# A MetaFormer block on one core: image loops written out, two biases folded into weights and outputs, the second norm derived from the first, and one probability product moved to GpSimd

## The chip, the core and the metric

The kernel runs on one core of a Trainium2 chip. A core has five engines that run side by side and meet at semaphores: TensorE (PE, its weight loads are PEld), VectorE (DVE), ScalarE (ACT), GpSimd (POOL) and SyncE (SP), which here issues transfers. The metric is the device time of one execution in microseconds (us). The time of the kernel before is the median of three runs.

## What is computed

Four images of 128 channels and 32 x 32 pixels pass through a token mixer with three attention branches and then through a mixture of eight experts, two for each token.

```python
# per image; xs is the layer-normed image as 1024 tokens x 128 channels, 4 heads
q_c, k_c, v_c = xs @ qkv_cmp_w + b                      # compressed branch
k_cmp = mlp(unfold(k_c, 4, stride 2) + pos_embed)       # 225 blocks of 16 pixels
v_cmp = mlp(unfold(v_c, 4, stride 2))
attn_cmp = softmax(q_c @ k_cmp.T * SCALE);  out_cmp = attn_cmp @ v_cmp @ proj + b
idx = top_k(attn_cmp.sum(heads).mean(queries), 16)      # selected branch: 16 of the blocks
attn_slc = softmax(q_s @ k_s[idx].T * SCALE); out_slc = attn_slc @ v_s[idx] @ proj + b
out_win = window_attention(x, 7 x 7 windows, bias table) # 25 windows of 49 pixels
out = g0 * out_cmp + g1 * out_slc + g2 * out_win         # g = sigmoid(mlp(xs))
# then, over all 4096 tokens: layer norm, router, layer norm of that again,
# the two best of 8 experts (128 -> 512 -> 128, gelu), weighted sum, residual
```

## The kernel before

**Structure.** Each engine has its own program. The mixer is worked off image by image. `attention` holds three stages: the compressed branch in 8 tiles of 128 queries against 225 keys (the `"c"` tiles), the windows together with the choice of the 16 blocks, and the selected branch in 8 tiles against 256 keys (the `"s"` tiles). `seam` joins two images: it finishes image b (outputs of the branches, their projection and gated sum, two norms, router, places of the tokens) and at the same time does the head of image b + 1 (norm, projections, the two block MLPs of keys and values, window values). The order is: the opening seam (head of image 0), then three times attention and seam, then attention and seam of the last image, then the experts, then the sum. In the kernel before, attention and seam of the images 0 to 2 are the body of a hardware loop (`Fori`) on each engine, and the last image is written out behind it. I count images from 0 here.

**A tile of attention.** TensorE makes the scores of tile t in two PSUM banks (L1354). VectorE takes the maximum (`maxima`, L887). ScalarE makes the exponentials with their sums (L668). VectorE takes the reciprocal (L894) and multiplies each head's 225 or 256 columns (`divide`, four instructions, L897). TensorE transposes the probabilities (L1272), VectorE and ScalarE each copy one half out (`first_chunk`, L912 in the selected branch, and L683), and two products a branch use the copies (L1297). The order on TensorE is scores(t), transposes(t - 2), and at t = 6 the first output product. The order on VectorE is `maxima(t)`, `divide(t - 1)`, `first_chunk(t - 2)`. The probabilities lie in a ring of three buffers.

**Banks.** A plan gives each PSUM result a bank and a turn. A wait on `bank_full` means that TensorE has filled it, a wait on `bank_read` that it has been copied.

**The seam.** The keys' MLP has 16 positions. VectorE adds the position's embedding to a strided view of the keys and writes it to `kp` (L1096, 16 instructions), and TensorE multiplies `kp` (L1481). The values' MLP reads the strided view of `vcT` directly (L1330). The window values get their bias on VectorE (L1059). `normalise` is statistics, their aggregate, a power on GpSimd (L552) and the scaling (L865). It runs three times in a middle seam: for the next image, for the tokens, and for the tokens once more. The last matrix step is the keys' second layer (L1514), which ScalarE copies to the block-diagonal `kbd` (L779). TensorE ends the seam with waits for all banks, and the first scores of the next image need `kbd`.

**GpSimd.** It does the window softmax's subtraction and product (L582, L589), part of the gather, the powers, and the 16 scatters of an image (L607), which stand at the end of its turn.

## Time and profile before

| | |
|---|---|
| median of three runs | 875.09 us (874.01 to 877.78) |
| the profiled execution, its own time | 872.5 us |
| span of its trace | 870.7 us |
| busy PE, DVE, ACT, POOL | 662.6, 594.7, 414.1, 240.5 us |
| images (from the opening to the last place of a token) | up to some 665 us |
| experts and sum | the rest |

The span is the trace from the first to the last instruction. The busy time of an engine is the sum over its instructions, and says nothing on whether the others wait for it. For that the trace lists, before each instruction, how long the engine was idle and who released it. "issue" stands for an idle time in which the profile shows nothing that the engine waited for.

### The profile page before, as it was taken

The page shows a single profiled execution, that of the slowest core. Times are in us where ns is not written, and L with a number is a line of the kernel's source. Part 1 is how long each engine was busy: PE and PEld are TensorE (multiplying, and loading weights), DVE is VectorE, ACT ScalarE, POOL GpSimd, SP SyncE. Part 2 cuts the span into 40 slices and gives each one's busy share as a digit, 9 for nine tenths or more (in the row PEclk, how much of TensorE's full clock was granted, in tenths as well). Part 3 has the DMA queues.
Part 4 walks back from the last instruction along what each step waited for, and adds up shares of the span by engine and source line. Part 5 has one row for each costly group of instructions (what it writes and reads, how often), then busy time and mean ns, then how long its engine had stood idle before and what let it go on. Part 6 is the DMA issues. An engine that isn't in the chain of part 4 may idle for free. (4 is left out here: it accounts for less than half of the span.)

```text
span 870.7 us, 18341 instructions
## 1 busy us (share of the span) xinstructions
PE 662.6 (76%) x4992; PEld 503.3 (58%) x4993; DVE 594.7 (68%) x1930; ACT 414.1 (48%) x1203; POOL 240.5 (28%) x399
## 2 busy tenths in 40 slices
PE   3997777799677769977767898776752299999953
PEld 2694353569434346954434597444342299999952
DVE  4647868788598879859787887886965044444424
ACT  1327437334463543427355423733701188887852
POOL 5000230200434001133400211531003455555540
PEclk9999969899899799989989999896975599999985
DMA  9700000000100000000000000100022122222236
GB/s 320 229 1 0 3 5 0 26 24 1 34 19 5 1 25 3 23 24 29 5 1 1 1 25 7 44 23 7 0 105 54 56 58 67 67 64 64 66 116 220
DMA packets 34225, 39.66 MB, mean 46 GB/s; under 512 B 11246, under 2 KB 26720, under 8 KB 33888
## 3 DMA queue, kind: packets, MB, share of 16 engines
q1 hardware_dynamic: 28592, 27.73, 10.4%
q0 software_dynamic: 4416, 9.00, 3.1%
q10 hardware_dynamic: 1152, 2.10, 0.7%
q8 instruction: 36, 0.59, 0.3%
q14 instruction: 29, 0.24, 0.1%
HBM read 25.38 MB, written 14.50 MB: 46 GB/s over the span
## 5 line engine op out<-in xcount | busy, mean ns | idle before, releaser
L668 ACT ACTIVATE r_P<-ps,nmx 128x225 f32<-128x225 f32 (+1 forms) x192 | 85.9, 465 | 56.7 <-DVE nmx L887 56.7
L804 ACT ACTIVATE R<-ps,R 128x128 f32<-128x128 f32 x292 | 83.5, 368 | 45.0 <-PE ps L1565 45.0
L887 DVE TENSOR_REDUCE nmx<-ps 128x4 f32<-128x900 f32 (+1 forms) x64 | 73.8, 1155 | 35.0 <-PE ps L1354 34.9
L1272 PE MATMUL ps<-ident,r_P 128*128 128x128 f32 (+1 forms) x384 | 58.0, 296 | 44.8 <-DVE r_P L897 36.5
L1354 PE MATMUL ps<-kbd,qT 64*128 64x450 f32 (+1 forms) x256 | 80.0, 729 | 16.0 <-issue 16.0
L607 POOL DMA_INDIRECT xs_d<-pay,pos x64 | 62.1, 970 | 103.0 <-DVE pos L1077 84.7
L1272 PEld LDWEIGHTS ps<-ident,r_P 128*128 128x128 f32 (+1 forms) x384 | 45.3, 155 | 75.9 <-DVE r_P L897 54.6
L643 POOL DMA_INDIRECT z_d<-R x72 | 69.4, 963 | 66.5 <-DVE R L1243 44.2
L552 POOL TENSOR_TENSOR rstd<-vpe,minus_half 128x8 f32<-128x8 f32 x12 | 19.8, 1650 | 238.8 <-DVE vpe L862 238.8
L1565 PE MATMUL ps<-R 128*128 128x128 f32 x584 | 79.2, 280 | 0.0
L1581 PE MATMUL ps<-fw_sb,R 128*128 x576 | 78.4, 279 | 0.0
L1565 PEld LDWEIGHTS ps<-R 128*128 128x128 f32 x584 | 72.7, 196 | 0.0
L1581 PEld LDWEIGHTS ps<-fw_sb,R 128*128 128x128 f32 x576 | 70.4, 193 | 2.3 <-issue 0.2
L1237 DVE TENSOR_TENSOR R<-ps,w1v_sb 128x128 f32<-128x128 f32 x72 | 21.0, 292 | 63.6 <-PE ps L1581 62.8
L897 DVE TENSOR_SCALAR r_P<-r_P,rZ 128x225 f32<-128x225 f32 (+1 forms) x192 | 54.6, 348 | 1.7
L796 ACT ACTIVATE R<-fw_sb 128x518 f32 x74 | 48.1, 650 | 12.7 <-DVE R L1219 12.6
L1330 PE MATMUL ps<-r_vc,w1v_sb 128*128 128x225 f32 x256 | 53.8, 367 | 0.0
L1403 PE MATMUL ps<-ident,r_P 113*49 113x113 f32 (+1 forms) x208 | 27.3, 279 | 32.3 <-POOL r_P L589 16.7
L1354 PEld LDWEIGHTS ps<-kbd,qT 64*128 64x128 f32 x256 | 27.5, 225 | 40.1 <-issue 37.3
L1481 PE MATMUL ps<-r_kp,w1k_sb 128*128 128x225 f32 x256 | 49.8, 354 | 1.1 <-DVE kbdw L412 1.1
L1330 PEld LDWEIGHTS ps<-r_vc,w1v_sb 128*128 128x128 f32 x256 | 47.6, 188 | 4.1
L1481 PEld LDWEIGHTS ps<-r_kp,w1k_sb 128*128 128x128 f32 x256 | 48.2, 190 | 1.6 <-issue 1.4
(208 smaller groups left out, 1348.4 us busy)
## 6 DMA issues: line engine op xcount, KB each, us to landing
R<-xs_d SPq DMA_DIRECT2D x76, 65.0 KB, 1.8
kbdw<-z_d SPq DMA_DIRECT2D x8, 512.0 KB, 5.7
x_sb<-x SPq DMA_DIRECT2D x4, 512.0 KB, 3.3
w1k_sb<-w1k SPq DMA_DIRECT2D x1, 2048.0 KB, 10.2
w1v_sb<-w1v SPq DMA_DIRECT2D x1, 2048.0 KB, 14.7
fw_sb<-fw SPq DMA_DIRECT2D x1, 2048.0 KB, 10.6
fw_sb<-fw SPq DMA_DIRECT2D x4, 512.0 KB, 11.3
t_d<-r_P SPq DMA_DIRECT2D x4, 512.0 KB, 2.6
```

What stands on the lines that cost most here:

```text
L607: gp.indirect_dma_start(xs_d, bass.IndirectOffsetOnAxis(pos[:, NT * k + t:NT * k + t + 1], 0), pay[:, k, t, :], None).then_inc(scattered, 16)
L643: gp.indirect_dma_start(z_d, bass.IndirectOffsetOnAxis(wd[:, r, 1:2].bitcast(U32), 0), yrow[:, r, :], None).then_inc(y_out[r], 16)
L668: last = sc.activation(Pb[t % NRING][:, h, 0:m], bank(ph, name)[:, (h % 2) * m:(h % 2) * m + m], ACT.Exp, bias=nmx[:, t % NRING, h:h + 1], ...
L804: last = sc.activation(hT[:, r % 2, c, :], hid(r)[:, C * c:C * c + C], ACT.Gelu, bias=wx[:, r, O_B1 + c:O_B1 + c + 1])
L887: ve.tensor_reduce(nmx[:, t % NRING, :].rearrange("p (a h) -> p a h", a=2), v.rearrange("p a (h m) -> p a h m", h=2), AX.X, ALU.max, negat ...
L897: last = ve.tensor_scalar(v, v, rZ[:, t % NRING, h:h + 1], None, ALU.mult)
L1272: last = tr(bank(ph, name)[0:m, k * j:k * j + k], src, ident[0:k, 0:k])
L1330: last = mm(bank(ph, f"mv{a}")[:, 0:NB], w1v_sb[:, s, C * a:C * a + C], vcT[:, r:r + 2 * NBH - 1:2, c:c + 2 * NBH - 1:2], start=(s == 0), ...
L1354: mm(bank(ph, name)[:, 0:2 * mk], qT[p0:p0 + 64, 128 * t:128 * t + 128], kbd[p0:p0 + 64, 2 * k:2 * k + 2, 0:mk], start=True, stop=True)\
L1481: last = mm(bank(ph, f"mk{a}")[:, 0:NB], w1k_sb[:, s, C * a:C * a + C], kp[:, s, :], start=(s == 0), stop=(s == NPOS - 1))
L1565: last = mm(hid(r)[:, C * c:C * c + C], wx[:, r, C * c:C * c + C], xe[:, r % 2, :], start=True, stop=True)
L1581: last = mm(outputs(r), hT[:, r % 2, c, :], fw_sb[:, bass.ds(e, 1), W1X + C * c:W1X + C * c + C].rearrange("p a n -> p (a n)"), start=(c = ...
```

## The change

- **Loops.** The loops over the images are written out on all five engines. The expert loop stays a loop.
- **Embedding.** The embedding's product with the keys' first layer is made once, in the opening seam (banks `pb` and `pc`), and added to the bias of that layer (`b1k`). `kp` goes, and the keys' MLP reads the strided keys.
- **Window values.** Their bias is added to the window outputs instead (each row of the probabilities sums to one), and ScalarE copies the values out.
- **Second norm.** The statistics of the second token norm are not taken. Its factor is worked out on GpSimd from the first (`second_inverse_root`), and VectorE multiplies by it.
- **Selected branch.** VectorE takes only the reciprocal, and GpSimd multiplies all four heads in one instruction (`scale_selected`).

```diff
+    fill("pb", when=head and not attention)
+    fill("mk0", "mk1", when=head)
+    fill("pc", when=head and not attention)
...
+            def second_inverse_root(k, b):
+                inverse_root(k)
+                pool.wait_ge(rstd_ready, k + 1)
+                gp.tensor_tensor(var2[:, 0, :], rstd[:, :], mv[:, :, 1], ALU.mult).then_inc(rstd2_step, 1)
+                pool.wait_ge(rstd2_step, 4 * b + 1)
+                gp.tensor_tensor(var2[:, 1, :], var2[:, 0, :], rstd[:, :], ALU.mult).then_inc(rstd2_step, 1)
+                pool.wait_ge(rstd2_step, 4 * b + 2)
+                gp.tensor_scalar(var2[:, 0, :], var2[:, 1, :], EPS_T, None, ALU.add).then_inc(rstd2_step, 1)
+                pool.wait_ge(rstd2_step, 4 * b + 3)
+                gp.tensor_tensor(rstd2[:, :], var2[:, 0, :], minus_half[:, :], ALU.pow).then_inc(rstd2_step, 1)
...
+            def scale_selected(b):
+                for t in range(NT):
+                    pool.wait_ge(rz_ready, b * NT + t + 1)
+                    v = Pb[t % NRING][:, :, 0:256]
+                    gp.tensor_tensor(v, v, rZ[:, t % NRING, :].unsqueeze(2).to_broadcast([128, HEADS, 256]),
+                                     ALU.mult).then_inc(prob_ready, 1)
...
-            with pool.Fori(0, B - 1) as b:
+            for b in range(B - 1):
                 windows(b)
-                head(middle_one(b), b + 1, 3 * b + 1)
-                inverse_root(3 * b + 2)
-                inverse_root(3 * b + 3)
+                scale_selected(b)
+                head(middle_one(b), b + 1, 2 * b + 1)
+                second_inverse_root(2 * b + 2, b)
                 scatter_rows(b)
...
+                    for g in range(NGRP):
+                        n = min(4, NWIN - 4 * g)
+                        act.wait_ge(*filled(ph, f"vw{g}"))
+                        sc.activation(vw[:, 4 * g:4 * g + n, :].rearrange("p w c -> p (w c)"),
+                                      bank(ph, f"vw{g}")[0:WTOK, 0:n * C], ACT.Copy).then_inc(read_sem(ph, f"vw{g}"), 1)
...
                     dve.wait_ge(*copied(ph, f"S{s}{t}b"))
+                    if s == "s":
+                        ve.reciprocal(rZ[:, t % NRING, :], Z[:, t % NRING, :]).then_inc(rz_ready, 1)
+                        return
...
-                            last = ve.tensor_copy(
+                            last = ve.tensor_scalar(
                                 owT[:, :].rearrange("p (r c) -> p r c", c=W)[:, r0:r0 + nr, c0:c0 + ncol],
...
-                                .rearrange("p (r c) -> p r c", r=WS)[:, 0:nr, 0:ncol])
+                                .rearrange("p (r c) -> p r c", r=WS)[:, 0:nr, 0:ncol], col("bv_w"), None, ALU.add)
...
-                    for s in range(NPOS):
-                        r, c = divmod(s, KS)
-                        ve.tensor_scalar(kp[:, s, :].rearrange("p (r c) -> p r c", r=NBH),
-                                         kcT[:, r:r + 2 * NBH - 1:2, c:c + 2 * NBH - 1:2],
-                                         cols[:, COL_POS + s:COL_POS + s + 1], None, ALU.add).then_inc(kp_ready, 1)
...
-                    normalise(norm + 1, xt_tok, pay[:, 0, :, 0:C], EPS_T, xn_ready)
+                    dve.wait_ge(rstd2_step, 4 * t_ + 4)
+                    for t in range(NT):
+                        last = ve.tensor_scalar(pay[:, 0, t, 0:C], xt_tok[:, t, :], rstd2[:, t:t + 1], None, ALU.mult)
+                    last.then_inc(xn_ready, 1)
...
+                    if t_ is None:
+                        pe.wait_ge(*free_for(ph, "pb"))
+                        for i in range(NPOS // 4):
+                            for j in range(4):
+                                s = 4 * i + j
+                                last = mm(bank(ph, "pb")[32 * j:32 * j + 32, 0:2 * C], cols[:, COL_POS + s:COL_POS + s + 32],
+                                          w1k_sb[:, s, :], start=(i == 0), stop=(i == NPOS // 4 - 1))
+                        last.then_inc(full_sem(ph, "pb"), 1)
...
                     for s in range(NPOS):
-                        pe.wait_ge(kp_ready, h * NPOS + s + 1)
+                        r, c = divmod(s, KS)
                         for a in range(2):
-                            last = mm(bank(ph, f"mk{a}")[:, 0:NB], w1k_sb[:, s, C * a:C * a + C], kp[:, s, :],
+                            last = mm(bank(ph, f"mk{a}")[:, 0:NB], w1k_sb[:, s, C * a:C * a + C],
+                                      kcT[:, r:r + 2 * NBH - 1:2, c:c + 2 * NBH - 1:2],
                                       start=(s == 0), stop=(s == NPOS - 1))
```

Three places show how the order of the instructions moves. The first is ScalarE where the loop over the images begins, between the copy to `kbd` and the first exponentials of an image. Before:

```order
L779 ACTIVATE kbd<-ps,cols 32x225 x3
L786 UNCONDITIONAL_BRANCH
L786 ISA
L665 ISA [waits t_stored]
L668 ACT_TABLE_LOAD
L668 ACTIVATE r_P,Z<-ps,nmx 128x225 [waits max_ready]
L668 ACTIVATE r_P,Z<-ps,nmx 128x225 x3
```

After, at the same place of the image (L813 is the copy to `kbd`, L696 the exponential, L807 the window values):

```order
L807 ACTIVATE r_vw<-ps 49x128 [waits bank_full1]
L813 ACTIVATE kbd<-ps,cols 32x225 [waits bank_full2]
L813 ACTIVATE kbd<-ps,cols 32x225 x3
L696 ACT_TABLE_LOAD [waits max_ready]
L696 ACTIVATE r_P,Z<-ps,nmx 128x225 [waits t_stored]
L696 ACTIVATE r_P,Z<-ps,nmx 128x225 x3
```

The branch is gone, and the load of the activation table now stands behind the wait for the first maximum, in all four images. In the kernel before it stands there in the last image only.

The second place is VectorE in the middle of the selected branch: two tiles before (L887 maximum, L894 reciprocal, L897 product, L912 copy of the transposed half).

```order
L887 TENSOR_REDUCE nmx<-ps 128x4 [waits bank_full1,bank_full0]
L894 RECIPROCAL rZ<-Z 128x4 [waits bank_read7]
L849 REGISTER_ALU
L897 TENSOR_SCALAR r_P<-r_P,rZ 128x256 [waits dve_done]
L897 TENSOR_SCALAR r_P<-r_P,rZ 128x256 x3
L912 COPY R<-ps 128x4x128 [waits bank_full3]
L883 REGISTER_ALU
L887 TENSOR_REDUCE nmx<-ps 128x4 [waits bank_full7,bank_full6]
L894 RECIPROCAL rZ<-Z 128x4 [waits bank_read1]
```

After, with L921 for the maximum, L929 for the reciprocal and L949 for the copy:

```order
L921 TENSOR_REDUCE nmx<-ps 128x4 [waits bank_full1,bank_full0]
L929 RECIPROCAL rZ<-Z 128x4 [waits bank_read7]
L949 COPY R<-ps 128x4x128 [waits bank_full3]
L921 TENSOR_REDUCE nmx<-ps 128x4 [waits bank_full7,bank_full6]
L929 RECIPROCAL rZ<-Z 128x4 [waits bank_read1]
```

The products are gone from VectorE, and the reciprocal of tile t - 1 still stands behind the maximum of tile t.

The third place is TensorE in the opening seam after the change, from the gate (L1500) over the new products (L1511, L1530) and the keys' MLP (L1520) to the values' MLP (L1359).

```order
L1500 MATMUL ps<-gw_sb,r_gh 128x3 x7
L1511 MATMUL ps<-w1k_sb,cols 32x256 [waits bank_read3,wk_in]
L1511 MATMUL ps<-w1k_sb,cols 32x256 x15
L1520 MATMUL ps<-r_kc,w1k_sb 128x225 [waits bank_read5,bank_read4]
L1520 MATMUL ps<-r_kc,w1k_sb 128x225 x31
L1530 MATMUL ps<-cols,pos_rows 128x1 [waits bank_read6,bank_read3]
L1530 MATMUL ps<-cols,pos_rows 128x1
L1359 MATMUL ps<-r_vc,w1v_sb 128x225 [waits bank_read7,bank_read6,wv_in]
```

Before, the keys' MLP stood directly behind the gate there, with a wait for `kp_ready` at each position.

## Rows read from the trace of the kernel before

**Rows 1.** The page: busy time, share of the span and count.

```profile
PE 662.6 (76%) x4992; PEld 503.3 (58%) x4993; DVE 594.7 (68%) x1930; ACT 414.1 (48%) x1203; POOL 240.5 (28%) x399
```

**Rows 2.** Waits of TensorE: who for whom, us in total, times, longest.

```profile
PE ps L1272 <- DVE r_P L897: 36.5, 37, 4.5
```

**Rows 3.** Timeline, image 0, entry of the loop: start, us, engine, line; idle before.

```profile
66.85 1.81 ACT L779 ACTIVATE kbd<-ps,cols 32x225 f32<-32x225 f32 x4 [6.10 <-PE ps L1514]
...
69.94 4.25 PE L1354 MATMUL ps<-kbd,qT 64*128 64x450 f32 x12 [2.25 <-issue]
...
98.49 0.15 DVE L964 TENSOR_REDUCE impcol<-impacc 97x1 f32<-97x8 f32 x1
```

**Rows 4.** Timeline, image 1, behind the first back edge.

```profile
222.47 1.80 ACT L779 ACTIVATE kbd<-ps,cols 32x225 f32<-32x225 f32 x4 [6.10 <-PE ps L1514]
...
229.63 2.73 PE L1354 MATMUL ps<-kbd,qT 64*128 64x450 f32 x6 [5.92 <-issue]
...
259.49 0.15 DVE L964 TENSOR_REDUCE impcol<-impacc 97x1 f32<-97x8 f32 x1
```

**Rows 5.** Timeline, image 3, written out behind the loop.

```profile
536.96 1.81 ACT L779 ACTIVATE kbd<-ps,cols 32x225 f32<-32x225 f32 x4 [6.10 <-PE ps L1514]
...
540.17 2.54 PE L1354 MATMUL ps<-kbd,qT 64*128 64x450 f32 x12 [1.98 <-issue]
...
542.53 1.28 ACT L668 ACT_TABLE_LOAD   x1 [3.77 <-DVE nmx L887]
...
571.70 0.15 DVE L964 TENSOR_REDUCE impcol<-impacc 97x1 f32<-97x8 f32 x1
```

**Rows 6.** Timeline of VectorE, image 1, selected branch, tiles 5 to 7.

```profile
302.96 1.22 DVE L887 TENSOR_REDUCE nmx<-ps 128x4 f32<-128x1024 f32 x1
304.09 0.17 DVE L894 RECIPROCAL rZ<-Z 128x4 f32<-128x4 f32 x1
304.29 1.14 DVE L897 TENSOR_SCALAR r_P<-r_P,rZ 128x256 f32<-128x256 f32 x4
305.35 0.68 DVE L912 COPY R<-ps 128x512 f32<-128x512 f32 x1
305.95 1.22 DVE L887 TENSOR_REDUCE nmx<-ps 128x4 f32<-128x1024 f32 x1
...
309.78 1.23 DVE L887 TENSOR_REDUCE nmx<-ps 128x4 f32<-128x1024 f32 x1 [0.76 <-PE ps L1354]
```

**Rows 7.** Timeline of TensorE in the same stretch.

```profile
299.51 1.09 PE L1272 MATMUL ps<-ident,r_gh 128*128 128x128 f32 x8 [0.57 <-DVE r_gh L897]
300.53 1.13 PE L1354 MATMUL ps<-kbd,qT 64*128 64x512 f32 x4
...
306.68 1.92 PE L1297 MATMUL ps<-R,v_sb 128*32 128x512 f32 x16
308.54 1.13 PE L1354 MATMUL ps<-kbd,qT 64*128 64x512 f32 x4
```

**Rows 8.** Timeline, image 1, windows: products of GpSimd, and TensorE behind one.

```profile
265.42 0.84 POOL L589 TENSOR_TENSOR r_P<-r_P,rZw 113x392 f32<-113x392 f32 x1 [5.00 <-DVE rZw L943]
...
284.75 0.51 POOL L589 TENSOR_TENSOR r_P<-r_P,rZw 49x196 f32<-49x196 f32 x1 [4.21 <-DVE rZw L943]
...
266.41 0.75 PE L1403 MATMUL ps<-ident,r_P 113*49 113x113 f32 x6 [1.58 <-POOL r_P L589]
```

**Rows 9.** Timeline of TensorE, second middle seam.

```profile
339.37 2.98 PE L1278 MATMUL ps<-xwin,qkvw_sb 128*128 128x245 f32 x8 [1.36 <-DVE r_vc L1101]
...
344.27 12.45 PE L1481 MATMUL ps<-r_kp,w1k_sb 128*128 128x225 f32 x64 [0.23 <-DVE kbdw L412]
```

**Rows 10.** Groups by line and shape: busy us, mean ns; idle before.

```profile
L1330 PE MATMUL ps<-r_vc,w1v_sb 128*128 128x225 f32 x256 | 53.8, 367 | 0.0
L1481 PE MATMUL ps<-r_kp,w1k_sb 128*128 128x225 f32 x256 | 49.8, 354 | 1.1 <-DVE kbdw L412 1.1
L1101 DVE TENSOR_SCALAR r_vc<-ps,cols 128x512 f32<-128x512 f32 x8 | 5.6, 740 | 0.0
```

**Rows 11.** Timeline, last seam: the router on TensorE, its reader on VectorE.

```profile
652.41 3.55 PE L1502 MATMUL ps<-wr_sb,R 128*128 128x8 f32 x16 [0.73 <-ACT R L763]
...
656.95 0.22 DVE L1140 TENSOR_TENSOR lg<-ps,rows 128x64 f32<-128x64 f32 x1
```

More of the change, by code:

```diff
@@ L300, in build @@
         vpe = sb("vpe", [128, NT])
+        var2 = sb("var2", [128, 2, NT])
+        rstd2 = sb("rstd2", [128, NT])
         gtok = sb("gtok", [128, NT, 3])
@@ L468, in store_t @@
                 sp.wait_ge(t_ready, b + 1)
-                sp.dma_start(t_d[bass.ds(b, 1), :, :].rearrange("a p n -> (a p) n") if not isinstance(b, int) else t_d[b, :, :],
-                             r_P[:, 0:N]).then_inc(t_stored, 16)
+                sp.dma_start(t_d[b, :, :], r_P[:, 0:N]).then_inc(t_stored, 16)
             sp.wait_ge(*filled(opening(), "xt1"))
             sp.dma_start(x_sb[:, :], x[1, :, :]).then_inc(x_in, 16)
-            with sp.Fori(0, B - 2) as b:
+            for b in range(B - 2):
                 select_tokens(b)
                 sp.wait_ge(*filled(middle_one(b), "xt1"))
-                sp.dma_start(x_sb[:, :], x[bass.ds(b + 2, 1), :, :].rearrange("a p n -> (a p) n")).then_inc(x_in, 16)
+                sp.dma_start(x_sb[:, :], x[b + 2, :, :]).then_inc(x_in, 16)
                 store_t(b)
@@ L621, in _ @@
             windows(B - 1)
[L622 to L623 removed]
+            scale_selected(B - 1)
+            second_inverse_root(2 * B - 1, B - 1)
             scatter_rows(B - 1)
@@ L655, in hidden_units @@
             def hidden_units(ph, name, a):
-                h, bias = {"mk": (hk, "b1k"), "mv": (hv, "b1v")}[name]
+                h, bias = {"mk": (hk, b1k[:, a:a + 1]), "mv": (hv, col(f"b1v{a}"))}[name]
+                act.wait_ge(*copied(opening(), "pc"))
                 act.wait_ge(*filled(ph, f"{name}{a}"))
                 sc.activation(h[:, a, :], bank(ph, f"{name}{a}")[:, 0:NB], ACT.Gelu,
-                              bias=col(f"{bias}{a}")).then_inc(read_sem(ph, f"{name}{a}"), 1)
+                              bias=bias).then_inc(read_sem(ph, f"{name}{a}"), 1)
             def attention(ph, b):
@@ L785, in _ @@
             seam(opening(), None, 0)
-            with act.Fori(0, B - 1) as b:
+            for b in range(B - 1):
                 attention(middle_one(b), b)
@@ L1052, in combine @@
                             link(last)
-            def values(ph):
-                for g in range(NGRP):
-                    n = min(4, NWIN - 4 * g)
-                    dve.wait_ge(*filled(ph, f"vw{g}"))
-                    ve.tensor_tensor(vw[:, 4 * g:4 * g + n, :],
-                                     bank(ph, f"vw{g}")[0:WTOK, 0:n * C].rearrange("p (w c) -> p w c", c=C),
-                                     rows[0:WTOK, ROW_BVW:ROW_BVW + C].unsqueeze(1).to_broadcast([WTOK, n, C]),
-                                     ALU.add).then_inc(read_sem(ph, f"vw{g}"), 1)
             def rows_of_picks(ph):
@@ L1170, in seam @@
                 if h is not None:
-                    values(ph)
                     dve.wait_ge(*filled(ph, "v2"))
@@ L1181, in _ @@
             assert links[1] == LINKS_FIRST, links
-            with dve.Fori(0, B - 1) as b:
+            for b in range(B - 1):
                 links[0], links[1] = LINKS_FIRST + b * LINKS_MIDDLE, 0
                 attention(middle_one(b), b)
-                seam(middle_one(b), b, b + 1, 3 * b + 1)
+                seam(middle_one(b), b, b + 1, 2 * b + 1)
                 assert links[1] == LINKS_MIDDLE, links
@@ L1188, in _ @@
             attention(closing(), B - 1)
-            seam(closing(), B - 1, None, 3 * B - 2)
+            seam(closing(), B - 1, None, 2 * B - 1)
             done = [0]
@@ L1484, in seam @@
                                 last.then_inc(full_sem(ph, f"mk{a}"), 1)
+                    if t_ is None:
+                        pe.wait_ge(*copied(ph, "pb"))
+                        pe.wait_ge(*free_for(ph, "pc"))
+                        for a in range(2):
+                            last = mm(bank(ph, "pc")[:, a:a + 1], pos_rows[:, C * a:C * a + C], col("quads"),
+                                      start=True, stop=True)
+                        last.then_inc(full_sem(ph, "pc"), 1)
                 if t_ is not None:
@@ L1541, in _ @@
             seam(opening(), None, 0)
-            with pe.Fori(0, B - 1) as b:
+            for b in range(B - 1):
                 attention(middle_one(b), b, b + 1)
```

36 lines of the change are left out of this document (22 added, 14 removed).

## The prediction

> **What bounds the kernel now.** I read the page first: TensorE is busy for 76% of the span and VectorE for 68% [rows 1], so no engine alone is the bound, and each stage has to be read from its own waits. The waits of TensorE come next: its largest single one, 36.5 us, is for the probability product of VectorE [rows 2]. Then I read the timelines at the joints between images. In image 1 the copy to `kbd` ends at 224.27 and TensorE issues the next scores at 229.63, 5.4 us later, with no releaser [rows 4]. In images 0 and 3, which do not stand behind a back edge, the same gap is 1.3 and 1.4 us [rows 3, 5]. In the selected branch a tile takes 2.99 us (from the maximum at 302.96 to the next at 305.95), and VectorE has no gap in it: maximum, reciprocal, four products, copy [rows 6]. In the seam TensorE runs the two block MLPs with almost no idle time [rows 9]. So there are three regimes: VectorE in the tiles, TensorE in the seams, a stall at the joints.
>
> **The joints.** I compare one stretch in the images: from the end of the `kbd` copy to the last instruction of the compressed branch (L964). It is 98.49 - 68.66 = 29.8 us in image 0 [rows 3], 35.2 in image 1 [rows 4] and 571.70 - 538.77 = 32.9 in image 3 [rows 5]. Image 3 is already straight-line code, so it is the pattern for all four after the change. It is slower than image 0 for a reason that the order of instructions shows: the table load of 1.28 us stands behind the first maximum, at 542.53 [rows 5]. Beside it TensorE idles longer in the fill, and the scatters of the image before run beside its tiles. After the change all four images have the load there. The gap of 1.4 us contains a branch in image 3 that will be gone. The waits for the banks stay, so I take 0.5 us, between 0.1 (a plain semaphore) and 1.4. That gives 32.0 us for images 1 to 3, and 31.3 for image 0, which has no scatters beside it: 29.8 and the load of 1.3, some 1.0 for the longer idle time, less 0.8 of gap. Images 1 and 2 save 3.2 each (I take image 2 like image 1), image 3 saves 0.9, and image 0 loses 1.5. Sum: **-5.8 us**, bounds -2.2 (gap as now) to -8.5.
>
> The Trainium skill (Runtime: NRT & Kernel Launch, Instruction fetch mechanics) says that a taken branch out of the loaded pages has to fetch its target before it can go on. By it the two gaps would fall wholly, some 10 us; it does not count the table load.
>
> **The selected branch.** Off VectorE: four products, 1.05 us of pitch a tile [rows 6]. Onto GpSimd: one product of 1024 columns. The trace has 392 columns in 0.84 and 196 in 0.51 us [rows 8], hence 1.7 ns a column, and 0.51 + 828 x 0.0017 = 1.9 us. Bounds: 1.5 (if long rows run some 25% faster than these short ones of 49) to 2.4.
>
> Does the tile get shorter? The orders decide. TensorE issues scores(t) only behind transposes(t - 3), and VectorE the reciprocal(t - 1) only behind maximum(t). So there is a ring of two tiles: transposes to scores 1.02 (299.51 to 300.53), scores to maximum 1.24 (308.54 to 309.78), maximum to reciprocal 1.13 [rows 6, 7], reciprocal and hop 0.25, product 1.9, hop to TensorE 0.15 (266.26 to 266.41 [rows 8]). The sum is 5.7, or 2.86 a tile. With the product on VectorE the same ring has 1.4 behind the start of the reciprocal instead of 2.3, that is 2.4 a tile, and VectorE's own work (2.99) decides. The tile thus gets only 0.1 us shorter, while the product's latency shows at both ends: the first transposes come 0.9 later, and so do the last. The output product at t = 6 (1.86 us, 306.68 to 308.54 [rows 7]) falls between transposes(4) and scores(7). Before, slack took up most of it: the last maximum comes 3.83 instead of 2.99 behind the one before (305.95 to 309.78 [rows 6]). Now it falls into the ring whole. I went through the eight tiles with these steps, each instruction at the later of its input and its engine. With the product on VectorE this gives 6.83 us from maximum(5) to maximum(7); the rows say 6.82. With the product on GpSimd the transposes of tiles 0, 5 and 7 come 0.9, 0.9 and 1.45 later than before. So the stage is 1.45 us longer, **+5.8 us** for four images. At a product of 1.5 us it is 0.3 shorter an image (-1), at 2.4 it is 3.5 longer (+14).
>
> The Trainium skill (GPSIMD Engine Reference, 3.1 Elementwise) speaks against this edit: it has 4497 ns for 2048 columns with two inputs. As an estimate from that page the product would take 2.3 us and the sum would be 7 us higher. This trace is below the page's pace (0.84 us for 392 columns), so I stay with the rows.
>
> **The seams.** In a middle seam `kp` (16 instructions of VectorE) goes, and with it TensorE's waits of 1.36 and 0.23 [rows 9]. The MLP now streams strided keys. The values' MLP does that already, at 367 against 354 ns [rows 10], so 64 instructions cost 0.8 more. Net -0.7, x3: **-2.1**. What else leaves VectorE here (statistics, a wait for GpSimd, window values) stood beside TensorE's back-to-back work and is worth nothing. The window values on ScalarE fill an idle time of 6.10 us ahead of `kbd` [rows 3 to 5]; without that cover they would cost seven copies of 512 columns, some 4 us at the 0.68 of VectorE's [rows 6]. In the opening seam the path is TensorE, and it gains the embedding products: 32 instructions of 256 columns into 32 rows each, like the 16 of 512 that take 1.92 [rows 7], so 1.9; 0.8 for the stride; 0.3 for the small products. Sum **+3.0**, bounds 1 and 9 (the upper one if the four strips don't overlap).
>
> **The last seam.** VectorE's second norm ends some 4 us earlier. But the next thing that it needs is the router's product, which ends at 655.96, and its reader starts at 656.95 now [rows 11]. So only 0.9 is left: **-0.9**, bounds 0 and -2.7 (if the router runs at the full TensorE clock). The places, scatters and experts behind it are unchanged.
>
> **Window outputs.** 25 copies an image get a column operand. From 512 columns the two forms cost 0.74 and 0.68 [rows 6, 10], so up to 0.06 each, 1.4 of VectorE. The stage is a relay between four engines; I take a third to be on the path, 0.45 an image, **+1.8**, bounds 0 and 5.6.
>
> **Sum:** -5.8 + 5.8 - 2.1 + 3.0 - 0.9 + 1.8 = +1.8, against the profiled execution's own 872.5, that is 874.3. The median of the runs shown lies 2.6 above it, so I predict **877 us**. About 0.5% (4.4 us) is what a measurement of this kernel can tell from no change.
>
> **Rivals.**
> - *GpSimd's product is quick (faster).* At 1.5 us the ring has slack, the branch gives -1 instead of +5.8, and with the gap at 0.1 us the joints give 1.6 more: 877 - 8.4, about 868. For it: the rows only show short rows of 49 columns. Against: the slope from two points. It decides below some 1.6 us.
> - *GpSimd's product is slow (slower).* At 2.4 us the branch costs +14 and the kernel takes about 885. For it: two inputs from SBUF over 1024 columns. Against: VectorE here reads PSUM, and nothing beside GpSimd stretched its 0.84 us.
> - *The joint isn't the branch.* If the 5.4 us stay in straight code, because loading the code itself is late, the joints only lose: 877 + 6 to 8, about 884. Against: image 3 shows 1.4 us.
> - Not in the cases: the half-clock spells of TensorE fall elsewhere. They may move the time by 3 us either way and are in the range.
>
> **Chances.** Forecast 0.44, quick product 0.25, slow product 0.23, stall that stays 0.08. The forecast's own range is 872 to 881; the range that holds 8 in 10 goes to the two products, 867 to 886. The quick product counts as faster, the slow one and the staying stall as slower, and the forecast as the same.
>
> **What would show it.** The new product on GpSimd at 1.9 us with a tile of 2.9 us in the selected branch, and VectorE waiting in it for scores; the first scores of an image within 0.5 us of `kbd`, with the table load behind the first maximum; no wait before L1520, whose mean is some 367 ns; a router reader that waits for TensorE. The forecast is wrong if a tile of the selected branch falls below 2.6 us or rises above 3.1.

## The result and the profile after

| | before | after |
|---|---|---|
| median, us (5 runs each, one chip) | 875.37 | 879.07 |
| lowest to highest, us | 874.01 to 877.78 | 878.43 to 881.55 |
| ratio (95% interval) | 1 | 1.0049 (1.0027 to 1.0071) |
| profiled execution: time, span, us | 872.5, 870.7 | 878.4, 876.4 |

The change costs some 0.5%, at the edge of what a measurement of this kernel tells from nothing; in a second group of runs (the control below) the ratio was 1.0069 (1.0042 to 1.0096). The page's line of busy time, beside [rows 1], has VectorE 77 us lower and GpSimd 64 higher:

```profile
PE 672.8 (77%) x5028; PEld 506.9 (58%) x5029; DVE 517.7 (59%) x1644; ACT 427.3 (49%) x1231; POOL 304.0 (35%) x443
```

**The joint** of image 0 after, on the timeline (start, us, engine, line; idle before in brackets), beside [rows 3]:

```profile
68.41 1.81 ACT L813 ACTIVATE kbd<-ps,cols 32x225 f32<-32x225 f32 x4 [0.43 <-PE ps L1562]
...
71.23 1.03 PE L1383 MATMUL ps<-kbd,qT 64*128 64x450 f32 x4 [1.98 <-issue]
...
73.58 1.28 ACT L696 ACT_TABLE_LOAD   x1 [3.37 <-DVE nmx L921]
...
102.31 0.15 DVE L1001 TENSOR_REDUCE impcol<-impacc 97x1 f32<-97x8 f32 x1
```

The gap behind `kbd` is 71.23 - 70.22 = 1.0 us (1.1 in image 1, 1.0 in the others), not 5.4, and not the 0.5 that I took. The table load is where it was expected. From here on I take the stretch from the end of `kbd` to the end of the importance column just before L1001, which is 0.1 behind the start of L1001 that the prediction took. It takes 32.2, 32.8, 32.7 and 32.7 us, against 29.9, 35.3, 35.2 and 33.0 before [rows 3 to 5]. TensorE's queue has the gap in it. One line's instructions, after, in the window 69 to 72 us:

```profile
L1586 PEldq EVENT_SEMAPHORE  x9: 51/51/51, 70.3 to 71.1; - x9
```

and the line of the back edge in the kernel before, with its durations in ns (least, median, most):

```profile
L1542 PEldq COMPARE_BRANCH  x3: 83/3802/3916, 225.6 to 540.0; - x3
L1182 DVEq COMPARE_BRANCH  x3: 59/63/72, 224.8 to 539.3; - x3
```

The first of the nine records is the wait for `kbd` itself, and eight more stand behind it in the seam's list of banks. All banks but that one have been free before, but each wait takes 0.11 us of the queue ((71.13 - 70.25) / 8). So of the 5.4 us before, 1.2 were waits and some 3.9 the taken branch of TensorE; the same branch cost VectorE 0.06. The branch that was not taken, behind the third image of the loop, took 0.08. A taken branch is not dear in itself: the back edge of the experts' loop, whose body has some 180 records of TensorE where the images' has some 2000, takes TensorE 0.21 to 0.25 us (the least, 0.083, is the one that was not taken):

```profile
L1571 PEldq COMPARE_BRANCH  x18: 83/215/248, 701.2 to 838.8; - x18
```

**The ring** of the selected branch, image 1 after, beside [rows 6, 7]. VectorE, then GpSimd, then TensorE:

```profile
303.49 1.23 DVE L921 TENSOR_REDUCE nmx<-ps 128x4 f32<-128x1024 f32 x1 [0.20 <-PE ps L1383]
304.63 0.18 DVE L929 RECIPROCAL rZ<-Z 128x4 f32<-128x4 f32 x1
305.44 0.69 DVE L949 COPY R<-ps 128x512 f32<-128x512 f32 x1 [0.62 <-PE ps L1301]
307.04 1.22 DVE L921 TENSOR_REDUCE nmx<-ps 128x4 f32<-128x1024 f32 x1 [0.91 <-PE ps L1383]
...
309.13 1.22 DVE L921 TENSOR_REDUCE nmx<-ps 128x4 f32<-128x1024 f32 x1 [0.21 <-PE ps L1383]
...
314.52 1.23 DVE L921 TENSOR_REDUCE nmx<-ps 128x4 f32<-128x1024 f32 x1 [2.76 <-PE ps L1383]
```

```profile
304.89 1.89 POOL L625 TENSOR_TENSOR r_P<-r_P,rZ 128x1024 f32<-128x1024 f32 x1 [0.20 <-DVE rZ L929]
308.42 1.89 POOL L625 TENSOR_TENSOR r_P<-r_P,rZ 128x1024 f32<-128x1024 f32 x1 [1.64 <-DVE rZ L929]
```

```profile
297.48 1.85 PE L1301 MATMUL ps<-ident,r_P 128*128 128x128 f32 x8 [2.27 <-POOL r_P L625]
299.26 2.00 PE L1383 MATMUL ps<-kbd,qT 64*128 64x512 f32 x4
301.19 1.10 PE L1301 MATMUL ps<-ident,r_P 128*128 128x128 f32 x8
302.22 1.13 PE L1383 MATMUL ps<-kbd,qT 64*128 64x512 f32 x4
```

The product takes 1.89 us, two tiles take 309.13 - 303.49 = 5.64, and VectorE waits for scores in the ring. What the rows also show is a cost that the prediction left out: the scores of 299.26 take 2.00 us where others take 1.13, because TensorE's clock was granted at half there (1.2 instead of 2.4 GHz, behind an idle time of 2.27 for GpSimd). From the first maximum of the branch to the last it takes 22.1 to 22.5 us in the four images, against 20.3 to 20.4 before.

The four stretches from the first selected scores to the first norm of the result, image by image, before and then after (us; busy us and count of each engine; PEclk, the granted share of TensorE's clock; DMA share, GB/s):

```profile
129.40:164.70 35.30, 26.88 (x182) 15.65 (x175) 28.23 (x80) 21.80 (x76) 0.00 (x0) 0.91 0.05 16
287.30:321.70 34.40, 27.00 (x178) 14.92 (x175) 28.21 (x81) 21.80 (x76) 0.00 (x0) 0.92 0.05 16
443.70:479.20 35.50, 26.96 (x179) 16.01 (x175) 28.21 (x81) 21.80 (x76) 0.00 (x0) 0.92 0.00 1
601.40:646.40 45.00, 31.03 (x199) 17.94 (x194) 35.43 (x104) 20.71 (x74) 0.00 (x0) 0.88 0.03 13
```

```profile
132.40:169.00 36.60, 27.96 (x178) 15.75 (x175) 20.19 (x49) 21.61 (x76) 15.10 (x8) 0.89 0.05 15
289.80:326.80 37.00, 27.80 (x180) 15.92 (x175) 20.25 (x49) 21.58 (x76) 15.10 (x8) 0.89 0.04 15
446.30:482.90 36.60, 28.04 (x182) 15.76 (x175) 20.24 (x48) 21.69 (x76) 15.10 (x8) 0.89 0.00 0
603.40:651.40 48.00, 32.86 (x198) 19.21 (x194) 27.41 (x73) 20.57 (x74) 15.10 (x8) 0.82 0.03 12
```

VectorE does 8 us less in each, and each is longer: by 1.3, 2.6, 1.1 and 3.0, 8.0 in all. The granted clock is lower in all four.

**The seams.** TensorE in the first middle seam and in the opening (then the keys' first product in the opening before), and the two forms of the block MLP:

```profile
189.33 13.41 PE L1520 MATMUL ps<-r_kc,w1k_sb 128*128 128x225 f32 x64
```

```profile
32.94 1.93 PE L1511 MATMUL ps<-w1k_sb,cols 128*32 128x256 f32 x32
...
34.81 0.47 PE L1520 MATMUL ps<-r_kc,w1k_sb 128*128 128x225 f32 x1
```

```profile
34.72 12.42 PE L1481 MATMUL ps<-r_kp,w1k_sb 128*128 128x225 f32 x64 [0.36 <-DVE kbdw L412]
```

```profile
L1359 PE MATMUL ps<-r_vc,w1v_sb 128*128 128x225 f32 x256 | 54.0, 367 | 0.0
L1520 PE MATMUL ps<-r_kc,w1k_sb 128*128 128x225 f32 x256 | 53.7, 368 | 0.0
```

No wait stands ahead of L1520, and its mean is 368 ns. In the last seam the router's reader waits for TensorE:

```profile
657.38 3.55 PE L1550 MATMUL ps<-wr_sb,R 128*128 128x8 f32 x16 [0.73 <-ACT R L791]
...
660.97 0.22 DVE L1170 TENSOR_TENSOR lg<-ps,rows 128x64 f32<-128x64 f32 x1 [3.15 <-PE ps L1550]
```

### The profile page after: what moved, and what is told of

Its sections match the earlier page's. It is cut to its first block, busy times and chain, and to the rows that moved or that the text cites. A ratio compares the mean times of both kernels' runs of the same rounds, so it can differ in the third digit from the quotient of the medians.

```text
span 876.4 us, 17293 instructions
## 1 busy us (share of the span) xinstructions
PE 672.8 (77%) x5028; PEld 506.9 (58%) x5029; DVE 517.7 (59%) x1644; ACT 427.3 (49%) x1231; POOL 304.0 (35%) x443
## 4 chain that ended last, share of the span: by engine, by line
PE 51%; DVE 21%; POOL 9%; issue 7%; DMA 5%; ACT 4%; POOLq 1%; SPq 1%; DVEq 0%; ACTq 0%
PE ps L1307 7%; PE ps L1520 6%; PE ps L1359 6%; PE ps L1301 5%; DVE nmx L921 5%; PE ps L1383 5%; PE ps L1629 4%; PE ps L1613 4%; PE ps L1326 3%; ACT r_P L696 3%; POOL r_P L625 3%; PE ps L1350 3%; DVE r_P L934 3%; DMA R<-xs_d 2%; POOL xs_d L634 2%
## 5 line engine op out<-in xcount | busy, mean ns | idle before, releaser
L696 ACT ACTIVATE r_P<-ps,nmx 128x225 f32<-128x225 f32 (+1 forms) x192 | 86.0, 466 | 53.5 <-DVE nmx L921 53.5
L1301 PE MATMUL ps<-ident,r_P 128*128 128x128 f32 (+1 forms) x384 | 62.6, 312 | 53.3 <-DVE r_P L934 26.1
L921 DVE TENSOR_REDUCE nmx<-ps 128x4 f32<-128x900 f32 (+1 forms) x64 | 73.7, 1156 | 49.1 <-PE ps L1383 49.0
L1301 PEld LDWEIGHTS ps<-ident,r_P 128*128 128x128 f32 (+1 forms) x384 | 49.4, 167 | 86.8 <-DVE r_P L934 38.1
L1383 PE MATMUL ps<-kbd,qT 64*128 64x450 f32 (+1 forms) x256 | 82.6, 752 | 6.8 <-issue 3.6
L625 POOL TENSOR_TENSOR r_P<-r_P,rZ 128x1024 f32<-128x1024 f32 x24 | 45.3, 1893 | 53.2 <-DVE rZ L929 53.2
L601 POOL TENSOR_TENSOR r_gh<-r_gh,nmw 113x392 f32<-113x392 f32 (+1 forms) x20 | 15.5, 773 | 111.5 <-DVE nmw L969 111.3
L1359 PE MATMUL ps<-r_vc,w1v_sb 128*128 128x225 f32 x256 | 54.0, 367 | 0.0
L1520 PE MATMUL ps<-r_kc,w1k_sb 128*128 128x225 f32 x256 | 53.7, 368 | 0.0
L1432 PE MATMUL ps<-ident,r_P 113*49 113x113 f32 (+1 forms) x208 | 26.7, 275 | 31.4 <-DVE R L1028 17.2
L1520 PEld LDWEIGHTS ps<-r_kc,w1k_sb 128*128 128x128 f32 x256 | 47.8, 188 | 4.9 <-issue 0.4
L1359 PEld LDWEIGHTS ps<-r_vc,w1v_sb 128*128 128x128 f32 x256 | 47.6, 188 | 4.2
L1257 DVE TENSOR_SCALAR R<-ps,R 128x128 f32<-128x128 f32 x74 | 30.2, 408 | 28.4 <-PE ps L1608 21.1
```

What stands on the lines that cost most here:

```text
L625: gp.tensor_tensor(v, v, rZ[:, t % NRING, :].unsqueeze(2).to_broadcast([128, HEADS, 256]), ALU.mult).then_inc(prob_ready, 1)
L696: last = sc.activation(Pb[t % NRING][:, h, 0:m], bank(ph, name)[:, (h % 2) * m:(h % 2) * m + m], ACT.Exp, bias=nmx[:, t % NRING, h:h + 1], ...
L921: ve.tensor_reduce(nmx[:, t % NRING, :].rearrange("p (a h) -> p a h", a=2), v.rearrange("p a (h m) -> p a h m", h=2), AX.X, ALU.max, negat ...
L1301: last = tr(bank(ph, name)[0:m, k * j:k * j + k], src, ident[0:k, 0:k])
L1359: last = mm(bank(ph, f"mv{a}")[:, 0:NB], w1v_sb[:, s, C * a:C * a + C], vcT[:, r:r + 2 * NBH - 1:2, c:c + 2 * NBH - 1:2], start=(s == 0), ...
L1383: mm(bank(ph, name)[:, 0:2 * mk], qT[p0:p0 + 64, 128 * t:128 * t + 128], kbd[p0:p0 + 64, 2 * k:2 * k + 2, 0:mk], start=True, stop=True)\
```

## The experiments

Ratios are to the kernel before, run on the same chip beside each group of four, with 95% intervals. The first two groups (e1 to e4; the control, e5 to e7) were on one chip, where the kernel before took 875.2 and 876.2 us; the third (e8 to e11) was on another, where it took 879.2. In the text below, "stretches" are those behind `kbd`, as defined under the joint. The "selected stretch" is that from the first selected scores to the norm, and the "windows' stretch" lies between the two.

### e1: the loops alone

```diff
-            with pe.Fori(0, B - 1) as b:        # and the same on SP, GpSimd, ScalarE, VectorE
+            for b in range(B - 1):
```

> The kernel before with nothing but its image loops written out. Joint theory (the prediction's own term, re-sized by the two traces): the five us without a releaser between the kbd copy and the first scores of images 1 and 2 are the branch back and go, the table load moves behind the first maximum, and some 1.0 us stays at each joint. The stretch from the kbd copy to the last importance column is then near 32.2 us in image 0 and 32.7 in the others, where the traces before have 29.9, 35.3, 35.2 and 33.0: 3.0 us less in all, so a time near 872.4. The prediction as written says 5.8 less, so 869.6. Rival (the joint is not the branch, code that is loaded for the first time is late): the gaps of 5.3 us stay and the time is that of the kernel before or above it.

Measured: 868.2 us, 0.9931 (0.9902 to 0.996). The stretches are 32.2, 32.6, 32.6 and 32.6, 3.4 us less in all, and a gap of 1.0 is left at each joint, so the branch was the greater part of the joint and the staying stall is refuted. The time fell by 6 to 7, not by 3.4. The profile puts the rest in the windows: 4.3 us less in the four images, of which the selected stretches give 1.1 back. In image 2 the windows' stretch takes 27.17 us instead of 27.68; in the loop TensorE's queue had 23 instructions of register arithmetic there and now has none. Images 0 and 3 gain 1.5 and 2.5 in it. They had been at half clock for longer before (granted clock 0.77 and 0.80, now 0.80 and 0.91), and why that fell out so is not shown.

### e2: the product back on VectorE

```diff
-                    if s == "s":
-                        ve.reciprocal(...).then_inc(rz_ready, 1)
-                        return
                     link(ve.reciprocal(rZ[:, t % NRING, :], Z[:, t % NRING, :]))
```

> The changed kernel with the selected branch's products back on VectorE, four of 256 columns a tile behind the reciprocal. Ring theory (GpSimd's product of 1.89 us makes a two-tile ring of 5.65 us and shows its whole latency at both ends): the pitch of a tile falls back to 2.99 us without the pattern of 2.4 and 5.1, first to last maximum takes 20.3 us instead of 22.1, first selected scores to the first norm 35.2 instead of 36.6; four images give 5.5 to 6 us, so 873 to 873.5. The two traces bear out up to 8.1 (the half-clock spells lie otherwise). Rival (the stage is bound by TensorE and its half-clock spells, the product is covered): less than 2 us, above 877. Rival (VectorE taken in again delays something else): also above 877.

Measured: 872.5 us, 0.9957 (0.9927 to 0.9986), against 1.005 and 1.007 for the changed kernel: some 8 to 10 us less, more than expected. (The two profiled executions differ by 4.4, and 4.1 of it lies in the selected stretches.) The pitch is 2.99 again and the pattern is gone. First to last maximum is 20.36 in image 0, but 21.4 in the others, where one tile takes 4.07 at half clock. So with the product on VectorE a half-clock spell is not hidden either. Both rivals fall.

### e3: the wait for k2 last

```diff
-                    for name in ("qc1", "k2", *(f"kw{i}" ...), *(f"qw{i}" ...), f"vw{NGRP - 1}", "v2"):
+                    for name in ("qc1", *(f"kw{i}" ...), *(f"qw{i}" ...), f"vw{NGRP - 1}", "v2", "k2"):
```

> The changed kernel, where TensorE waits for the reader of k2 (the kbd copy) last of the ten waits at the end of a seam and not second. Wait-chain theory (the 1.0 us left at a joint is eight to nine waits of TensorE's queue, one after the other at 0.106 us, that stand behind the one that is really late): the first scores start 0.2 to 0.3 us behind the kbd copy, 0.75 earlier four times over, so 3.0 less: 876.1. Rival (what stays at the joint is the latency from ScalarE's write to TensorE's start): no change, 879.1, gap still 1.0.

Measured: 874.4 us, 0.9981 (0.9947 to 1.0015). Line, then timeline, at the first joint:

```profile
L1586 PEldq EVENT_SEMAPHORE  x2: 51/51/51, 70.3 to 70.7; - x2
```

```profile
68.86 1.80 ACT L813 ACTIVATE kbd<-ps,cols 32x225 f32<-32x225 f32 x4 [0.43 <-PE ps L1562]
...
70.80 1.40 PE L1383 MATMUL ps<-kbd,qT 64*128 64x450 f32 x6 [1.11 <-ACT kbd L813]
```

`kbd` ends at 70.66 and TensorE starts at 70.80. The gap is 0.14 at all four joints, which is the semaphore alone. The stretches are 31.4, 31.7, 31.8 and 31.4, 0.8 to 1.3 shorter. So of the 1.0 us some 0.85 was the chain of eight waits, and the order of a list is worth 4 us here in the stretches and 3.8 in the spans (872.6 for 876.4); the ratios say 6 to 8.

### e4: the table load ahead

```diff
                     hidden_units(ph, "mv", 1)
+                    sc.activation(warm[:, :], cols[:, 0:1], ACT.Exp)
```

> The changed kernel with one more activation of ScalarE, an exponential of one column that nobody reads, behind the last hidden units of a seam, so that the table load stands there, in an idle time of some 4 us, and not behind the first maximum of an image. Table theory: the first four exponentials come 1.28 us earlier in each image, VectorE and TensorE follow at once since the fill of the tiles is a relay, 1.0 to 1.3 an image, so 4 to 5 us less: 874 to 875. It also accounts for the 1.3 that image 0 was to lose. Rival (the ring of the compressed branch makes it up, VectorE's work of a tile sets the pace and the late start is caught up within the tiles): under 1.5 less, above 877.5.

Measured: 874.0 us, 0.9989 (0.9956 to 1.0022). The stretches fall to 29.6, 31.0, 30.2 and 31.4, by 8.1 in all where 5 at most was expected: an exponential that is 1.28 late goes with up to 2.6. In image 0 the granted clock of the stretch is also 0.94 where it was 0.84, so not all of the 2.6 need be the load. The selected stretches of images 1 and 2 are 38.3 and 38.9, longer than in the profile of the change alone (37.0, 36.6). But the control below, which is the changed kernel itself, has 39.4 and 38.4 there, so this is no effect of the edit that can be told from chance.

### The control, and e5: the product shared out

```diff
+                        for h in range(2):      # VectorE, behind its reciprocal
+                            last = ve.tensor_scalar(v, v, rZ[:, t % NRING, h:h + 1], None, ALU.mult)
-                    v = Pb[t % NRING][:, :, 0:256]
+                    v = Pb[t % NRING][:, 2:HEADS, 0:256]      # GpSimd
```

> The changed kernel itself, so that the others of this group stand beside it on one chip. Ratio to the kernel before near 1.005, as in the result; the first group of experiments stood beside the kernel before alone, and a value between 1.002 and 1.008 here lets their differences to the changed kernel be read from their ratios.

> The changed kernel with the selected branch's product shared out: heads 0 and 1 on VectorE (two of its products), heads 2 and 3 on GpSimd (one product of 512 columns). Ring theory: GpSimd's part takes near 1.05 us (between 0.84 for 392 columns and 1.89 for 1024), the two-tile ring is 1.02 + 1.24 + 1.14 + 0.25 + 1.05 + 0.15 = 4.85 us instead of 5.65, and VectorE's own work 2.99 - 0.53 = 2.46 a tile; so tiles of 2.45 us, first to last maximum 18.5 to 19.5 us instead of 22.1, and with the shorter end 3.5 to 4.5 us an image: 14 to 18 in all, near 863. Rival (VectorE and GpSimd hinder each other when both work on the probabilities of one tile): the halves stretch above 0.35 and 1.3 us, and the tile stays near 2.8. Rival (TensorE or ScalarE set the tile once VectorE is down): ScalarE's four exponentials with their sums and its copy take some 2.5 us a tile, so it could not fall below that.

Measured: the control 881.2 us, 1.0069 (1.0042 to 1.0096); e5 883.9, 1.0095 (1.0072 to 1.0117). My ring theory was wrong by 21 us here. VectorE, then GpSimd, in tiles 4 and 5 of image 0:

```profile
151.21 0.16 DVE L929 RECIPROCAL rZ<-Z 128x4 f32<-128x4 f32 x1
151.41 1.49 DVE L933 TENSOR_SCALAR r_P<-r_P,rZ 128x256 f32<-128x256 f32 x2
152.82 0.68 DVE L954 COPY R<-ps 128x512 f32<-128x512 f32 x1
153.42 1.21 DVE L921 TENSOR_REDUCE nmx<-ps 128x4 f32<-128x1024 f32 x1
```

```profile
151.45 1.04 POOL L625 TENSOR_TENSOR r_P<-r_P,rZ 128x512 f32<-128x512 f32 x1 [2.30 <-DVE rZ L929]
```

GpSimd's half takes the 1.04 us that was expected. But VectorE's first product, begun at 151.41, does not end before GpSimd's does: it takes 1.23 instead of 0.35, and the second 0.34 as ever. It is so in all 32 tiles. The tile costs VectorE 3.35 us instead of 2.99. The first rival holds for VectorE's half (GpSimd's did not stretch): GpSimd's product from SBUF to SBUF stops VectorE's. Maxima and copies out of PSUM are not touched (1.21 and 0.68), and beside the whole product on GpSimd VectorE has only those. The Trainium skill (SBUF — State Buffer, Who interferes with whom) has this as a port pair of VectorE and GpSimd that one of them holds for a whole instruction. The traces agree in that the split fails and the whole product does not. They do not agree with the page on who is held: it says that whoever issues first gets the pair, and here VectorE's product begins 0.04 us before GpSimd's in all 32 tiles and is the one held.

### e6 and e7: both joint edits, without and with the folding

e6 is e1 with the edits of e3 and e4. e7 is e2 with them.

> The kernel before with its image loops written out, the wait for the reader of k2 last at the end of a seam, and the exponential of one column ahead of the window values; nothing folded and no product on GpSimd. If the three parts add up: 868.2 as in the unrolled kernel, less 4 x 0.85 for the waits (their chain came out at 0.14 instead of 0.99), less some 4 x 1.0 for the table load: 861, ratio 0.984. Rival (the half-clock spells of TensorE give it back, as image 1 of the kernel with the early table load suggests, 31.0 us against 29.6 in image 0): above 865.

> The changed kernel with the product back on VectorE and the same two edits (wait for k2 last, table load ahead). It differs from the run before in this list by the folded embedding and biases, the second norm and the window values alone. The prediction's terms for these (-2.1 seams, +3.0 opening, -0.9 last seam, +1.8 window outputs) say 1.8 slower. The traces after re-size them: seams 3 x (-2.3 + 1.0), opening near +0.3 since a wait for the shifted keys of 1.9 us goes there too, last seam -0.9, window outputs 0: 4.5 faster. The first group's times say 4.3 slower (872.5 with these parts, 868.2 without). So near 866 if the folding costs by the streaming of strided keys and by the half-clock spells, near 857 if the re-sized terms hold.

Measured: e6 861.4 us, 0.9847 (0.9821 to 0.9873); e7 859.6, 0.9806 (0.9781 to 0.983). The parts add up in e6 to the microsecond (861 expected), and the rival falls. What was folded is worth 1.8 us by these two, while e2 against e1 said 4.3 the other way. Both differences are within the intervals of their ratios together, so its sign stays open; the spans of the two profiled executions, 857.2 and 857.6, don't decide it either.

### e8 to e11: one chip, one edit each

e8 is the kernel of e7 again. e9 puts the product on GpSimd, as the change does. e10 stores even and odd columns apart:

```diff
+        kcP = r_kc[:, :].rearrange("p (f r c) -> p f r c", f=2, r=H)      # vcP alike
-                                      kcT[:, r:r + 2 * NBH - 1:2, c:c + 2 * NBH - 1:2],
+                                      kcP[:, c % 2, r:r + 2 * NBH - 1:2, c // 2:c // 2 + NBH],
```

e11 has `tensor_copy` in place of `tensor_scalar` at the window outputs, which leaves out the window values' bias.

> The kernel of e7_folded_joint_table again, unchanged, as the one that the other three of this group are read against on one chip: ratio to the kernel before 0.978 to 0.983.

> The kernel of e8_fixed_joint_again with the selected branch's product on GpSimd, as in the changed kernel. Each theory is about the price of this one edit with the joints out of the way. The prediction's term: 1.45 us an image, 5.8 in all, ratio 0.007 higher (0.9876). The two profiles of the changed kernel against that with the product on VectorE say 4.4 and 5.6; the medians of the first group against the control of the second say 8 to 9, which would need TensorE to spend more time at half clock in this stage (the pattern of 2.1 and 5.4 us idles it longer at a time). Rival: with the table load out of the way the ring has slack and the edit costs under 3.

> The kernel of e8_fixed_joint_again with keys and values stored as even and odd columns apart (ScalarE and VectorE write every second place), so that the block MLPs' 512 products read rows of 15 neighbouring columns instead of every second one. Stride theory: the 13 ns that such a product takes longer than one of 225 neighbouring columns (367 against 354) are for the step of two inside a row; they fall away for keys and values, 512 x 13 = 6.7 us less, ratio 0.0077 lower, if the writers don't stretch. Rival (the 13 ns are for 15 separate rows, or for any two-dimensional reading): 367 stays, no change of the time; and writers with a step may cost 0.1 to 0.7 us each (16 of them, beside TensorE's work).

> The kernel of e8_fixed_joint_again with plain copies at the window outputs, without the column operand; this leaves out the window values' bias. The prediction put 0.45 us an image on it, 1.8 in all (ratio 0.002, below what five rounds tell); its upper bound of 5.6 would show as 0.0065. The traces say 0: the stretch from the importance columns to the selected scores takes 27.63 us in image 2 after and 27.68 before. What can be read surely is the mean of one such operation: if the operand costs 0.06 us each, 248 ns falls below 200.

| | us | ratio (95%) |
|---|---|---|
| e8 | 858.7 | 0.9796 (0.9752 to 0.9839) |
| e9, product on GpSimd | 867.9 | 0.9893 (0.9856 to 0.993) |
| e10, columns apart | 846.0 | 0.9635 (0.9597 to 0.9672) |
| e11, no window bias | 857.6 | 0.9781 (0.9744 to 0.9819) |

**e9.** The product on GpSimd costs 9.2 us in the medians and 9.0 in the spans. Selected stretches of e8, then of e9 (columns as above):

```profile
132.09:166.53 34.44, 26.73 (x178) 15.16 (x175) 28.48 (x81) 21.80 (x76) 0.00 (x0) 0.93 0.05 16
283.70:319.19 35.49, 27.34 (x178) 15.95 (x175) 28.57 (x80) 21.80 (x76) 0.00 (x0) 0.90 0.05 16
434.94:469.38 34.44, 27.14 (x178) 15.26 (x175) 28.48 (x81) 21.80 (x76) 0.00 (x0) 0.92 0.00 1
```

```profile
131.32:166.66 35.34, 25.25 (x178) 14.80 (x175) 20.20 (x49) 21.47 (x76) 15.12 (x8) 0.96 0.04 16
284.01:323.28 39.27, 30.70 (x168) 17.41 (x165) 20.09 (x49) 21.79 (x76) 15.11 (x8) 0.76 0.04 14
439.49:478.48 38.99, 30.68 (x178) 16.98 (x175) 20.21 (x49) 21.69 (x76) 15.11 (x8) 0.80 0.00 0
```

In image 0, where the clock was granted at 0.96, the edit costs 0.9 us. In images 1 and 2, at 0.76 and 0.80, it costs 3.8 and 4.5; in image 3, at 0.92, nothing (44.9 and 45.0). So the latency alone is at most 0.9, and the larger part goes with the half clock, which here comes in the ring or in the output products behind it. The other profiles bear the size out: the four selected stretches sum to 158.1 to 161.1 us in the five profiles with the whole product on GpSimd (the change, the control, e3, e4, e9) and to 149.3 to 154.1 in the eight with it on VectorE. Whether TensorE's waits for GpSimd bring the half clock about is not shown; no run moves the one without the other. TensorE in image 2 of e9, at the end of the tiles:

```profile
466.96 1.09 PE L1303 MATMUL ps<-ident,r_P 128*128 128x128 f32 x8 [1.58 <-POOL r_P L626]
469.05 1.97 PE L1303 MATMUL ps<-ident,r_P 128*128 128x128 f32 x8 [1.00 <-POOL r_P L626]
471.76 3.64 PE L1328 MATMUL ps<-R,v_sb 128*32 128x256 f32 x32 [0.73 <-issue]
```

TensorE idles for GpSimd twice. The transposes then take 1.97 instead of 1.09 and the output products 3.64 instead of 1.93 (which they take in image 1 of the changed kernel), 1.2 instead of 2.4 GHz.

**e10.** The groups by shape of the block MLP and of its two writers:

```profile
L1360 PE MATMUL ps<-r_vc,w1v_sb 128*128 128x225 f32 x256 | 50.1, 354 | 0.0
L1521 PE MATMUL ps<-r_kc,w1k_sb 128*128 128x225 f32 x256 | 49.6, 354 | 0.0
...
L769 ACT ACTIVATE r_kc<-ps,cols 128x512 f32<-128x512 f32 x8 | 8.3, 1143 | 14.4 <-PE ps L1308 14.4
L1121 DVE TENSOR_SCALAR r_vc<-ps,cols 128x512 f32<-128x512 f32 x8 | 8.2, 1108 | 5.8 <-PE ps L1308 5.8
```

The products are back at 354 ns, so the 13 ns are the step of two inside a row and not the 15 rows. The writers stretch from 0.69 and 0.75 to 1.14 and 1.11, beside TensorE's work, and cost nothing. The span is 6.5 shorter than that of e8, as the stride theory says (6.7). The median is 12.7 shorter; the intervals of the two ratios allow from 9 to 19, and what that has beyond the 6.7 I can't name. (The profiled execution of e10 is the slowest of its six, 851.9 us, so its span is not that of the median.)

**e11.** The operand costs what the prediction took. The shape of 49 columns has a mean of 258 ns after the change and of 198 without the operand:

```profile
L1060 DVE COPY r_vc<-ps 128x49 f32<-128x49 f32 x64 | 9.7, 198 | 5.6 <-PE ps L1440 5.6
```

The windows' stretch in images 2 and 3 takes 27.18 us, against 27.67 and 27.72 in e8: 0.5 an image. My reading "the traces say 0" was wrong. The 0.5 had been hidden by as much that the end of the register arithmetic gives (e1: 27.17).

## Why the prediction came out

877 was forecast and 879.07 measured, in the range of 867 to 886, and "the same" was a close call. That it came so near is in part luck, since the terms miss by up to 2.8 us and in both directions. The sum of +1.8 was low: between the two profiled executions lie 878.4 - 872.5 = 5.9 us. The median of after stands only 0.6 above its profiled execution, not 2.6, and that took 2 us back. By its terms, in the stretches of the two spans (the middle seams are read from the norm to the first product of the values' MLP, the opening to the end of `kbd`; the measured terms sum to the 5.7 us between the spans):

| term | forecast | measured |
|---|---|---|
| joints | -5.8 | -3.0 |
| selected branch | +5.8 | +8.0 |
| middle seams | -2.1 | -3.3 |
| opening seam | +3.0 | +1.6 |
| last seam | -0.9 | -0.9 |
| window outputs | +1.8 | +1.6 |
| behind the scatters | 0 | +1.7 |

- **The joints.** The step "the waits for the banks stay, so I take 0.5 us, between 0.1 and 1.4" was mis-sized: 1.0 stands there, a hop of 0.14 and eight waits at 0.11. That is 2.1 of the missing 2.8. Another 0.3 is image 0, where I had 2.3 for the table load and the idle time with it, and e4 shows up to 2.6; the remaining 0.4 lies in the other images. That the branch was the stall is shown (e1, and the row of 3.9 us). Together with the register arithmetic of the windows, of which I had no term, the loops alone gave 6 to 7 us, so -5.8 was right in size for the loops by luck: the joints are half of it.
- **The selected branch.** Product 1.9 (measured 1.89), ring 5.7 (5.64), and the whole of the output product in the last pitches (5.39 from 309.13 to 314.52): right. The ring is confirmed as the mechanism, but the term was too small, because I priced it at the full clock. The latency itself was taken too large (1.45 us an image, against the 0.9 of e9 at a clock of 0.96), and some 4 an image stand where the granted clock is 0.76 to 0.80. The half-clock spells that I set aside as "not in the cases" belong in this term, whatever brings them about. The bound "the forecast is wrong if a tile rises above 3.1" was put on the wrong number: over the whole branch it is 22.1 / 7 = 3.16, the ring alone 2.82.
- **The seams.** The stride was sized right (0.96 a seam for 0.8). The middle seams gained 1.2 us more than forecast: where the clock is full up to the keys' first product, a seam takes 34.5 us instead of 35.8, and the second of them gained nothing at a granted clock of 0.92 there. The opening cost 1.4 less than forecast. In it I left out what I had counted in the others, TensorE's waits behind VectorE's shifted keys: the first keys' product starts at 34.81, with 1.93 of embedding products ahead of it, where it had started at 34.72.
- **Last seam, window outputs.** Right, and for the reasons given (router row; e11, 0.06 an operation and 0.5 an image). That the windows' stretches differ by 1.6 in the sum is chance: of the 1.6, image 1 alone has 2.4, at a granted clock of 0.85 for 0.91, and the half clock moves them by more.
- **Behind the scatters** no instruction was changed, and 1.7 us more were spent. It is hardly chance: from the start of the last scatter to the end it takes 185.4 to 185.9 us in the three profiles without the folded parts (before, e1, e6) and 186.8 to 188.6 in the eleven with them. A turn of the experts' loop takes some 0.1 us longer there. I have no cause for it, but it belongs to the price of the folding.
- **The rivals.** Quick and slow product fell with 1.89 us, the staying stall with e1. That the half-clock spells "may move the time by 3 us either way" was too small for the selected branch alone: by the 0.9 of e9, an estimate, some 4.4 of its 8.0 us go with them.

The version that is fastest is e10: unrolled, folded, product on VectorE, wait for k2 last, table load ahead, columns apart. It takes 846.0 us, 0.9635 of the kernel before.

## What to carry to other kernels

Work taken off an engine that is "the bound" of a stage brings nothing if the same work, on another engine, stands in the loop of waits between tiles: add up that loop with the new latency first, and price it at the low clock too, if TensorE stands in it. In a list of waits put the wait whose event comes last at the end, and issue the load of an activation table where the engine idles. Read what a strided operand costs per instruction and pay it once, in the writer, if the writer stands beside other work.

## What the runs showed of the hardware

- A wait in TensorE's queue takes 0.11 us even when its semaphore has long been there.
- The taken back edge of the images' loop cost TensorE 3.8 to 3.9 us and VectorE 0.06; that of the experts' loop cost TensorE 0.21 to 0.25. The Trainium skill's rule that the prediction cites (Runtime: NRT & Kernel Launch, Instruction fetch mechanics) would explain the two prices of TensorE, by the length of the body. Why VectorE's loop, with some 580 records a turn, does not pay, no run here tells.
- Beside a GpSimd product from SBUF, VectorE's product of 256 columns from SBUF takes 1.23 us instead of 0.35; its maxima and copies from PSUM keep their times.
- A product over 225 columns in every second place takes 367 ns, over rows of 15 neighbours 354. Writing 512 columns to every second place takes 1.1 us instead of 0.7.
